# The last top-2 expert stage of a twelve-sublayer decoder: half the tokens routed earlier, fixed regions per expert

## The chip, the cores and the metric

The kernel runs on one core of a Trainium2 chip. The metric is the device time of one execution in microseconds (us); lower is better. Three runs of the kernel before took 828.32, 831.12 and 840.23 us, median 831.12 us.

## The reference

Four decoder layers of three sublayers each work on 1024 tokens (16 sequences of 64) of 128 features in float32; after each sublayer comes `x = layernorm(x + sublayer(x))`. The last two sublayers matter here: a 16-head cross attention (`x3` in the kernel), and a mixture of eight experts with two chosen per token:

```python
logits = xt @ Wg.T                                   # (1024, 8)
topk_logits, topk_idx = jax.lax.top_k(logits, 2)
w = jax.nn.softmax(topk_logits, axis=-1)
gates = jnp.zeros((T, N_EXPERTS)).at[rows, topk_idx].add(w)
h = gelu(einsum('th,ehi->tei', xt, W1) + b1)         # 128 -> 512 per expert
o = einsum('tei,eih->teh', h, W2) + b2               # 512 -> 128
y = einsum('te,teh->th', gates, o)
```

## The kernel before, in words

Tokens lie in eight tiles of 128 (tile t holds tokens 128t to 128t+127). Every sublayer is a chain of small steps per tile, each a few instructions on one engine: in `x3`, `v`/`q`/`k` project, `sc` scores, `ex` exponentiates, `tu` and `pt` transpose and copy back, `va` applies values (PE), `on` normalises (DVE), `fo` and `o` transpose the result, `y` is the output projection (PE), `re` adds the residual and takes its statistics (DVE), `rs` makes the reciprocal deviation (POOL), `fi` normalises (DVE), `x` transposes the new tile for the next stage (PE, then a copy on ACT). A planner (`chain_plan`) writes the order of these steps for each engine ahead of time; the change adds steps at fixed places of that order and moves none of the planner's own. Engines execute their list in order and meet by semaphores; a wait holds everything behind it on that engine.

The last expert stage (`top2_ffn` on each engine) then runs as follows. PE makes the router's logits (`logits`: one 128x8 matmul per tile; tiles 0 to 6 in one go just ahead of the last `x`, tile 7 behind it). DVE copies them, picks the first and second expert per token (`choose_first`, twice), and PE counts by matmuls with a triangular and an all-ones matrix how many tokens of each expert come before each token. DVE turns the counts into places (`slot3`), packed so that each expert's tokens start at a multiple of 128 behind the expert before. For that it needs the total counts of all tokens. POOL then scatters the token rows to DRAM (`slots3_x`): 16 indirect DMAs of 128 rows, each row 128 features and a row number. SP waits for all of them and loads the rows back as 23 blocks of 128 rows (three DMAs), and the row numbers in a fourth. DVE reads the 23 owners of the blocks into registers (`value_load`), and stages each block's weights by a register address (`fetch`, two copies). PE runs per block one transpose, four `up` matmuls and four `down` matmuls (each float32 matmul shows twice in the trace), ACT applies Gelu between, DVE copies the result, POOL scatters it to its tokens (`back3_y`). At the end SP loads those rows, and DVE and ACT add and normalise.

Ahead of this, long before it is used, SP zeroes the rows of `slots3_x` and later writes the row numbers of empty places into its last column; small tables that the ranks need are made by DVE in the middle of the program (`rank_tables`).

## Time and profile before

| what | value |
|---|---|
| profiled execution | 832.95 us; its span 831.0 us |
| busy: PE, PE weight loads, DVE, ACT, POOL | 679.0, 523.0, 586.3, 460.9, 435.3 us |
| mean granted PE clock | 0.869 |
| `x3` ends (last tile transposed) | 727.6 us into the span |
| scatters of the last stage | 736.8 to 758.2 us |
| first transposition of a loaded block | 761.0 us |
| expert loop | 761.0 to 811.2 us |
| rest: rows back, sum, normalisation, output | to 831.0 us |

Times of events count from the span's start. A busy PE is not a PE at its peak. In a timeline row, merged neighbours of one kind show as "x4"; idle time in brackets is the engine's own before that row, and what ended it. "issue" is time in which the engine waited for nothing that the profile shows.

### The profile page before, as it was taken

The numbers are of one execution on the slowest core, as the hardware profiler recorded it, in microseconds if no ns is written. First come the engines' busy times: TensorE is split into PE (matmuls) and PEld (weight loads), VectorE is DVE, ScalarE is ACT, GpSimd is POOL, SyncE is SP. The second block draws the span as 40 slices with busy tenths as digits, with TensorE's granted clock in tenths as the row PEclk, the third lists the DMA queues.
The fourth block names the chain that finished last, engine by engine and source line by source line (L and its number), as shares of the span: only waits on it lengthen the run. The fifth ranks groups of instructions, "written<-read, shape, count | busy, mean of one in ns | idle before, by whom it ended". The sixth has DMA issues, their size and how long they took to land.

```text
span 831.0 us, 21693 instructions
## 1 busy us (share of the span) xinstructions
PE 679.0 (82%) x8146; PEld 523.0 (63%) x8146; DVE 586.3 (71%) x1576; ACT 460.9 (55%) x1141; POOL 435.3 (52%) x579
## 2 busy tenths in 40 slices
PE   5888968899989996999967999859688899833990
PEld 2566625767867784777635776629565677622990
DVE  4876859799798765888568989435469789641554
ACT  2235737587876654877524765337347657322661
POOL 3268736677556532443327876135566667343450
PEclk8668968799999998999986999579889999855996
DMA  8068000000000000000019100031225460004002
GB/s 337 9 230 123 2 1 2 1 2 1 2 2 2 1 2 1 3 3 2 3 2 251 55 4 2 2 97 42 67 93 158 155 213 3 2 26 100 30 36 85
DMA packets 50804, 44.67 MB, mean 54 GB/s; under 512 B 15408, under 2 KB 41136, under 8 KB 50192
## 3 DMA queue, kind: packets, MB, share of 16 engines
q1 hardware_dynamic: 48464, 38.70, 16.8%
q0 software_dynamic: 2240, 4.60, 1.6%
q8 instruction: 67, 1.10, 0.6%
q14 instruction: 33, 0.27, 0.1%
HBM read 30.94 MB, written 12.36 MB: 52 GB/s over the span
## 4 chain that ended last, share of the span: by engine, by line
PE 49%; DVE 19%; POOL 9%; issue 9%; ACT 5%; DMA 5%; SPq 1%; DVEq 0%; ACTq 0%; POOLq 0%
PE bank L839 5%; PE bank L818 5%; PE bank L827 4%; PE bank L854 3%; PE bank L1002 3%; PE bank L1060 3%; PE bank L1067 3%; PE bank L910 2%; DVE pairs L1584 2%; DVE pairs L1580 2%; POOL slots_x L1955 2%; PE bank L887 2%; POOL sm L1897 2%; DMA rel_scratch<-G 2%; PE bank L749 1%
## 5 line engine op out<-in xcount | busy, mean ns | idle before, releaser
L1897 POOL TENSOR_TENSOR sm<-sm,mx 128x512 f32<-128x512 f32 x80 | 83.8, 1049 | 44.0 <-DVE mx L1534 43.4
L1158 ACT COPY pT<-bank 128x512 f32<-128x512 f32 x112 | 65.3, 583 | 38.4 <-PE bank L827 37.0
L1153 ACT ACTIVATE pr<-sm 128x512 f32<-128x512 f32 x112 | 70.1, 632 | 25.3 <-POOL sm L1897 24.4
L1892 POOL TENSOR_TENSOR pairs<-KS,quad 128x512 f32<-128x512 f32 x56 | 59.9, 1072 | 36.4 <-ACT KS L1135 36.4
L827 PE MATMUL bank<-W,pr 128*128 128x128 f32 x448 | 72.1, 285 | 8.1 <-ACT pT L1158 6.6
L1868 POOL TENSOR_SCALAR veps<-mv 128x1 f32<-128x1 f32 x104 | 25.1, 241 | 99.3 <-DVE mv L1469 99.2
L818 PE MATMUL bank<-pairs,Q 64*128 64x256 f32 x448 | 67.1, 420 | 2.0 <-DVE sm L1519 1.0
L839 PEld LDWEIGHTS bank<-VX,pT 64*64 64x64 f32 x3584 | 60.1, 139 | 13.0 <-issue 7.4
L839 PE MATMUL bank<-VX,pT 64*64 64x9 f32 (+1 forms) x3584 | 65.0, 203 | 2.4 <-ACT pT L1158 1.2
L1869 POOL TENSOR_TENSOR rstd<-veps,W 128x1 f32<-128x1 f32 x104 | 60.6, 583 | 8.7
L827 PEld LDWEIGHTS bank<-W,pr 128*128 128x128 f32 x448 | 51.0, 144 | 20.3 <-issue 10.9
L1534 DVE TENSOR_REDUCE mx<-sm 128x8 f32<-128x512 f32 x80 | 54.9, 686 | 2.8
L1168 ACT COPY XT<-bank 128x128 f32<-128x128 f32 x72 | 19.1, 266 | 58.6 <-PE bank L749 58.3
L1473 DVE TENSOR_SCALAR X<-res,mv,rstd 128x128 f32<-128x128 f32 x76 | 39.5, 520 | 15.2 <-POOL rstd L1869 14.9
L818 PEld LDWEIGHTS bank<-pairs,Q 64*128 64x128 f32 x448 | 41.2, 195 | 13.4 <-issue 7.2
L1141 ACT ACTIVATE Q<-bank,bqm,W 128x128 f32<-128x128 f32 x96 | 38.9, 458 | 9.1 <-PE bank L802 8.8
L887 PE MATMUL bank<-big,HT 128*128 128x512 f32 x64 | 38.3, 696 | 6.5 <-ACT big L1185 4.4
L749 PE MATMUL bank<-W,X 128*128 128x128 f32 x88 | 30.5, 347 | 14.1 <-DVE X L1473 13.1
L1531 DVE TENSOR_TENSOR sm<-bank,cap 128x512 f32<-128x512 f32 x48 | 32.8, 684 | 6.6 <-PE bank L818 6.0
L854 PE MATMUL bank<-WO,oT 128*64 128x128 f32 x384 | 34.6, 303 | 1.9 <-ACT oT L1162 1.4
L1912 POOL TENSOR_TENSOR big<-pairs 128x512 f32<-128x512 f32 x16 | 22.7, 1416 | 23.1 <-DVE pairs L1584 23.1
L1584 DVE TENSOR_TENSOR pairs<-big 128x512 f32<-128x512 f32 x32 | 32.5, 1015 | 0.0
(355 smaller groups left out, 1869.7 us busy)
## 6 DMA issues: line engine op xcount, KB each, us to landing
big<-gup SPq DMA_DIRECT2D x4, 1024.0 KB, 10.1
rel_scratch<-G SPq DMA_DIRECT2D x16, 256.0 KB, 2.9
W<-small SPq DMA_DIRECT2D x1, 3206.5 KB, 12.2
big<-early SPq DMA_DIRECT2D x2, 1557.0 KB, 8.4
slots_x<-zero SPq DMA_DIRECT2D x2, 1472.0 KB, 24.9
big<-down SPq DMA_DIRECT2D x8, 256.0 KB, 8.8
QM<-rel_scratch SPq DMA_DIRECT2D x16, 128.0 KB, 2.7
PM<-rel_scratch SPq DMA_DIRECT2D x16, 128.0 KB, 2.8
```

The costliest lines, as they stand in the source:

```text
L818: last = mm(ps[r][:, b * 256:(b + 1) * 256].rearrange("p (g k) -> p g k", g=4), Q[rows, q2 + b, :, :].rearrange("p c q -> p (c q)"), keys( ...
L827: last = pe.transpose(tile(ps, p), pr[:, u % 2, 4 * h + p, :, :].rearrange("p b k -> p (b k)"), ident)
L839: last = mm(ps[b][m, p * blk:(p + 1) * blk], pT[r, u % 2, p, m], V[r, 16 * s_ + 2 * p + c, :], start=True, stop=True)
L854: last = mm(ps[b * S:(b + 1) * S, 0:P], oT[:, t % 2, c * S:(c + 1) * S], WO[:, a["i"] % 4, b, c, :], start=(c == 0), stop=(c == 1))
L887: mm(fill(b_[0], (q_raw, k_raw)[i])[:, :], h, early_w(f"f{l}.wqkv", 512 * i, 512 * i + 512), start=True, stop=True).then_inc((fq_full, fk_ ...
L1153: act.activation(pr[:, u % 2, 4 * h:4 * h + 4, :, :].rearrange("p g b k -> p b g k"), sm[:, 2 * (u % 2) + h, :].rearrange("p (b g k) -> p ...
L1158: act.copy(pT[:, u % 2, 4 * h:4 * h + 4, :], bank[BK[f"tu{h}"]][:, :].rearrange("p (h n) -> p h n", h=4)).then_inc(pt_ready, 1)
L1534: dve.tensor_reduce(top, dst, AX.X, ALU.max).then_inc(mx_ready, 1)
L1584: return tt(M2[:, i, :].rearrange("p (h c d) -> p h c d", h=8, c=2), swapped, bc(table, [P, 8, 2, 32], 1), ALU.mult)
L1869: tt(rstd[:, i, :], veps[:, i, :], power, ALU.pow).then_inc(rstd_ready, 1)
L1892: tt(keys(u), bc(KS[:, u % 4, :], [P, 4, P], 1), bc(quad, [P, 4, P], 2), ALU.mult).then_inc(k_split, 1)
L1897: tt(v, v, bc(mx[:, slot, :], [P, 8, S], 2), ALU.subtract).then_inc(pcentered, 1)
```

## The change

The second experts' rows go to fixed regions, and the first four tiles are routed ahead.

- Each expert gets a fixed region of 1024 rows in `slots3_x` (11,136 rows with the spare ones; 2,944 before), so a place is `1024 * expert + rank` and needs no total. Places, row numbers and the filling grow with it: 87 blocks of 128 rows are zeroed and numbered where 23 were. Five DVE instructions are added to the tables in the middle of the program.
- Tiles 0 to 3: PE makes their logits behind `v` of tile 6 of `x3`, ACT copies them to SBUF behind the last `ex`; DVE picks the first expert behind `fi` of tile 4 (six instructions) and the second behind `v` of tile 7 (five); PE ranks them behind `x` of tile 5 by nine matmuls; DVE makes their eight columns of places behind `re` of tile 6 (three). POOL sends the first scatter behind `rs` of tile 6 and seven more behind `rs` of tile 7. ACT makes the two copies of each token tile right behind each `x` of `x3`, not in the last stage.
- Tiles 4 to 7 follow as before in `top2_ffn`, at half the size: a running sum over all choices (one scan of 128x128) and three rank matmuls; three DVE instructions make the places, and POOL sends the last eight scatters. A fourth matmul gives the totals, from which 12 DVE instructions make the blocks' owners and the address of each block's first row.
- SP reads 23 addresses into registers, and then issues 23 DMAs of 128 rows (row number included) in six groups with a semaphore each, where there were three and one for the numbers.
- DVE's 23 register loads are spread: five ahead of the sum with the experts' bias, seven behind it, eleven in the loop. ACT loads the Gelu table right behind the softmax's exponential.

PE's order at the end of `x3`, before; L749 is `x`, L846 `fo`, L854 `y`, L981 the logits:

```order
L749 MATMUL bank<-W,X 128x128 [waits o_ready,x_ready]
L846 MATMUL bank<-W,OB 128x128 [waits xt_ready,on_ready]
L854 MATMUL bank<-WO,oT 64x128 [waits y_used,wo_in,o_ready]
L854 MATMUL bank<-WO,oT 64x128 x3
L749 MATMUL bank<-W,X 128x128 [waits o_ready,x_ready]
L981 MATMUL bank<-W,XT 128x8 [waits on_ready,xt_ready]
L981 MATMUL bank<-W,XT 128x8 x6
L749 MATMUL bank<-W,X 128x128 [waits xt_ready,x_ready]
```

and with the change (L767 is `x`, L903 to L909 the early ranks, L864 `fo`, L872 `y`):

```order
L767 MATMUL bank<-W,X 128x128 [waits o_ready,x_ready]
L903 MATMUL bank<-QM,tri 128x64 [waits lg_ready,one_ready]
L908 MATMUL bank<-QM,ones 128x7x8
L908 MATMUL bank<-QM,ones 128x6x8
L908 MATMUL bank<-QM,ones 128x5x8
L908 MATMUL bank<-QM,ones 128x4x8
L908 MATMUL bank<-QM,ones 128x3x8
L908 MATMUL bank<-QM,ones 128x2x8
L908 MATMUL bank<-QM,ones 128x8
L909 MATMUL bank<-base,W 128x64
L864 MATMUL bank<-W,OB 128x128 [waits xt_ready,on_ready]
L872 MATMUL bank<-WO,oT 64x128 [waits y_used,wo_in,o_ready]
```

Between `x` of tile 5 and `fo` of tile 7 stand nine matmuls, and of the logits three tiles' are left further on instead of seven's.

SP's queue behind the experts' weights, before:

```order
L679 DMA big<-e3w 128x4x128 x4
L650 DMA pr<-slots_x 128x4x128 [waits scattered]
L650 DMA pr<-slots_x 128x12x128
L650 DMA sm<-slots_x 128x7x128
L651 DMA token_of<-slots_x 128x23x1
L687 DMA X<-back_y 128x4x128 [waits y_stored]
```

and with the change, from the last two of 23 register loads to the second of 23 block loads:

```order
L696 ISA x2
L696 TENSOR_LOAD first
L696 ISA x2
L700 REGISTER_ALU [waits scattered]
L700 DMA pr<-slots_x 128x129
L700 REGISTER_ALU
L700 DMA pr<-slots_x 128x129
```

The wait for the scatters now stands behind all 23 register loads, and each DMA behind a register operation.

POOL's order at the end of `x3`, before (L1868 and L1869 are `rs`):

```order
L1868 TENSOR_SCALAR veps<-mv 128x1 [waits var_ready]
L1869 TENSOR_TENSOR rstd<-veps,W 128x1 [waits pool_link]
L1955 DMA slots_x<-XB_id,slot 2944x129 [waits xs_ready,e3_in,slot_ready]
L1955 DMA slots_x<-XB_id,slot 2944x129 [waits xs_ready] x7
L1955 DMA slots_x<-WO,slot 2944x129 [waits xs_ready] x8
L1960 DMA back_y<-pT,token_of 4992x128 [waits block_ready,token_in]
```

and with the change (L1974 and L1975 are `rs`):

```order
L1974 TENSOR_SCALAR veps<-mv 128x1 [waits var_ready]
L1975 TENSOR_TENSOR rstd<-veps,W 128x1 [waits pool_link]
L2020 DMA slots_x<-XB_id,slot 11136x129 [waits xs_ready,e3_in,slot_ready]
L1974 TENSOR_SCALAR veps<-mv 128x1 [waits var_ready]
L1975 TENSOR_TENSOR rstd<-veps,W 128x1 [waits pool_link]
L2020 DMA slots_x<-VX,slot 11136x129 [waits xs_ready]
L2020 DMA slots_x<-XB_id,slot 11136x129 [waits xs_ready]
```

One scatter moved between `rs` of tiles 6 and 7; seven more follow with no wait for places.

```diff
+ROWS3 = NE3 * TOK + BLOCKS3 * P
+EARLY3 = MT // 2
+XG_GROUPS = [0, 1, 2, 3, 6, 10, BLOCKS3]
...
-    slots3_x = nc.dram_tensor("slots3_x", (BLOCKS3 * P, P + 1), F32, kind="Internal").ap()
-    back3_y = nc.dram_tensor("back3_y", (2 * TOK + BLOCKS * P, P), F32, kind="Internal").ap()
+    slots3_flat = nc.dram_tensor("slots3_x", (ROWS3 * (P + 1),), F32, kind="Internal").ap()
+    slots3_x = slots3_flat.rearrange("(r n) -> r n", n=P + 1)
+    back3_y = nc.dram_tensor("back3_y", (2 * TOK + ROWS3, P), F32, kind="Internal").ap()
...
+        XK = [VX32[:, :, :, :].rearrange("p a h d -> p (a h d)")[:, 0:EARLY3 * (P + 1)].rearrange("p (t n) -> p t n", t=EARLY3),
+              HT[:, :, :].rearrange("p b k -> p (b k)")[:, 0:EARLY3 * (P + 1)].rearrange("p (t n) -> p t n", t=EARLY3)]
+        hot = one[:, :, :].rearrange("p a b -> p (a b)").rearrange("p (e t k) -> p t k e", e=NE3, k=2)
+        XG3 = [pr[:, :, :, :, :].rearrange("p z i b k -> p (z i b k)")[:, i * (P + 1):(i + 1) * (P + 1)] for i in range(15)] + [
+            sm[:, :, :].rearrange("p z n -> p (z n)")[:, i * (P + 1):(i + 1) * (P + 1)] for i in range(BLOCKS3 - 15)]
...
-            sp.dma_start(slots3_x[:, 0:P].rearrange("(i p) n -> p i n", p=P), bc(zero[:, :], [P, BLOCKS3, P], 1)).then_inc(e3_in, 16)
+            sp.dma_start(slots3_x[:, 0:P].rearrange("(i p) n -> p i n", p=P), bc(zero[:, :], [P, ROWS3 // P, P], 1)).then_inc(e3_in, 16)
...
-            sp.dma_start(slots3_x[:, P:P + 1].rearrange("(i p) n -> p i n", p=P), token_of[:, 0:BLOCKS3].unsqueeze(2),
+            sp.dma_start(slots3_x[:, P:P + 1].rearrange("(i p) n -> p i n", p=P), fill3[:, :].unsqueeze(2),
...
+            sp.wait_ge(slot_ready, 5)
+            first = [sp.value_load(first3[0:1, j:j + 1], min_val=0, max_val=(ROWS3 - P) * (P + 1)) for j in range(BLOCKS3)]
             sp.wait_ge(scattered, 16 * MT * 3)
-            slots_in(slots3_x, BLOCKS3)
+            for j in range(BLOCKS3):
+                group = [j >= a for a in XG_GROUPS[1:]].count(True)
+                sp.dma_start(XG3[j], slots3_flat[bass.ds(first[j], P * (P + 1))].rearrange("(p n) -> p n", n=P + 1)).then_inc(xg3_in[group][0], 16)
...
+                        if name == "x3" and t == EARLY3 - 1:
+                            early_at = due.now(said)
+                        if name == "x3" and t == EARLY3 + 1:
+                            early_ranks()
+                    if step == "v" and name == "x3" and t == MT - 2:
+                        early_logits(early_at)
+            def early_logits(x_at):
+                pe.wait_ge(xt_ready, x_at)
+                ps = fill(0, lg_ready)
+                for t in range(EARLY3):
+                    last = mm(ps[:, t * NE3:(t + 1) * NE3], tile(XT, t), w("e3.r"), start=True, stop=True)
+                last.then_inc(logit_full, 1)
+            def early_ranks():
+                pe.wait_ge(one_ready, 3)
+                due(slot_ready)
+                ps = fill(0, slot_ready)
+                ranks = ps[:, 0:EARLY3 * NE2].rearrange("p (e t k) -> p e t k", e=NE3, k=2)
+                mm(ranks, tri[:, :], hot[:, 0:EARLY3, :, :].rearrange("p t k e -> p e t k"), start=True, stop=False)
+                ranks = ps[:, 0:EARLY3 * NE2].rearrange("p (e m) -> p m e", e=NE3)
+                for m in range(2 * EARLY3 - 1):
+                    n = 2 * EARLY3 - 1 - m
+                    own = hot[:, m // 2, m % 2, :]
+                    mm(ranks[:, m + 1:, :], ones[:, :], bc(own, [P, n, NE3], 1), start=False, stop=False)
+                mm(ps[:, 0:EARLY3 * NE2].rearrange("p (e m) -> p e m", e=NE3), ident, bc(base3[:, :], [P, NE3, 2 * EARLY3], 2),
+                   start=False, stop=True).then_inc(rank_full, 1)
...
-                pe.wait_ge(one_ready, 3)
-                due(slot_ready)
+                pe.wait_ge(one_ready, 4)
                 ps = fill(7, slot_ready)
-                chosen = one[:, :, :].rearrange("p t (k e) -> p e k t", k=2)
-                ps = ps[:, 0:2 * P].rearrange("p (i e k t) -> p i e k t", i=2, e=NE3, k=2)
-                mm(ps[:, 0, :, :, :], tri[:, :], chosen, start=True, stop=True)
-                mm(ps[:, 1, :, :, :], ones[:, :], chosen, start=True, stop=True).then_inc(rank_full, 1)
-                pe.wait_ge(one_ready, 4)
+                own = slice(2 * EARLY3, 2 * MT)
+                incl = two[:, :, :].rearrange("p a b -> p (a b)").rearrange("p (e m) -> p e m", e=NE3)
+                ranks = ps[:, 0:(MT - EARLY3) * NE2].rearrange("p (e m) -> p e m", e=NE3)
+                mm(ranks, ident, bc(base3[:, :], [P, NE3, 2 * (MT - EARLY3)], 2), start=True, stop=False)
+                mm(ranks, ones[:, :], incl[:, :, own], start=False, stop=False)
+                mm(ranks.rearrange("p e (t k) -> p e t k", k=2), trim[:, :], hot[:, EARLY3:MT, :, :].rearrange("p t k e -> p e t k"),
+                   start=False, stop=True).then_inc(rank_full, 1)
+                mm(fill(5, slot_ready)[:, 0:NE3], ones[:, :], incl[:, :, 2 * MT - 1], start=True, stop=True).then_inc(rank_full, 1)
+                pe.wait_ge(one_ready, 5)
...
+                        if name == "x3":
+                            act.copy(XB[:, t, :], X[:, t, :]).then_inc(xs_ready, 1)
+                            act.copy(XK[t // EARLY3][:, t % EARLY3, 0:P], X[:, t, :]).then_inc(xs_ready, 1)
+                    if step == "ex" and name == "x3" and t == MT - 1 and h == 1:
+                        act.wait_ge(logit_full, 2)
+                        act.copy(lg[:, 0:EARLY3, 0:NE3], bank[0][:, 0:EARLY3 * NE3].rearrange("p (t e) -> p t e", t=EARLY3)).then_inc(lg_ready, 1)
...
-                for t in range(MT):
-                    act.copy(XB[:, t, :], X[:, t, :]).then_inc(xs_ready, 1)
-                act.wait_ge(lg_ready, 3)
+                act.wait_ge(lg_ready, 5)
                 act.activation(col[:, 4, :], col[:, 3, :], ACT.Exp).then_inc(score_ready, 1)
-                for t in range(MT):
-                    act.copy(XK[:, t, 0:P], X[:, t, :]).then_inc(xs_ready, 1)
+                act.preload_act_table_set("gelu_and_others")
                 for hh in range(2):
...
+                link(tt(trim[:, :], tri[:, :], ones[:, :], ALU.subtract))
+                link(ts(base3[:, :], w("down8"), -float(TOK), float(TOK * NE3 - 1), ALU.mult, ALU.add))
+                link(dve.tensor_tensor_scan(fill3[:, :], ones[:, 0:ROWS3 // P], ones[:, 0:ROWS3 // P], 0.0, ALU.mult, ALU.add))
+                link(ts(fill3[:, :], fill3[:, :], float(P), upward[:, :], ALU.mult, ALU.add))
+                ts(fill3[:, :].bitcast(I32), fill3[:, :], float(TOK - P), None, ALU.add)
...
+                    if name == "x3":
+                        if step == "fi" and t == EARLY3:
+                            early_first()
+                        if step == "v" and t == MT - 1:
+                            early_second()
+                        if step == "re" and t == MT - 2:
+                            early_slots()
+            early = slice(0, EARLY3)
+            def early_first():
+                l8, one8 = lg[:, early, 0:NE3], hot[:, early, 0, :]
+                dve.wait_ge(lg_ready, 2)
+                link(choose_first(one8, l8, NE3, w("down8"), early, 2))
+                stt(l8, one8, -BIG, l8, ALU.mult, ALU.add).then_inc(lg_ready, 1)
+            def early_second():
+                dve.wait_ge(lg_ready, 3)
+                choose_first(hot[:, early, 1, :], lg[:, early, 0:NE3], NE3, w("down8"), early).then_inc(one_ready, 1)
+            def early_slots():
+                n = EARLY3 * NE2
+                place = sig[:, :, :].rearrange("p a b -> p (a b)")[:, 0:n]
+                by_e = lambda v: v.rearrange("p (e t k) -> p e t k", e=NE3, k=2)
+                dve.wait_ge(rank_full, 2)
+                link(tt(by_e(place), by_e(bank[0][:, 0:n]), hot[:, early, :, :].rearrange("p t k e -> p e t k"), ALU.mult))
+                link(dve.tensor_reduce(slotf[:, 0:2 * EARLY3], place.rearrange("p (e m) -> p m e", e=NE3), AX.X, ALU.add))
+                dve.tensor_copy(slot3[:, 0:2 * EARLY3], slotf[:, 0:2 * EARLY3]).then_inc(slot_ready, 1)
...
+                dve.tensor_tensor_scan(flat(two[:, :, :]), flat(newrow[:, :, :]), flat(one[:, :, :]), 0.0, ALU.mult,
+                                       ALU.add).then_inc(one_ready, 1)
                 tt(col[:, 3, :], col[:, 0, :], col[:, 2, :], ALU.subtract).then_inc(lg_ready, 1)
...
+                link(tt(start_of, over, bc(until, [P, BLOCKS3, NE3], 1), ALU.mult))
...
+                firstf = token_of[:, 0:BLOCKS3]
+                link(dve.tensor_reduce(firstf, start_of, AX.X, ALU.max))
+                link(tt(firstf, steps24[:, 0:BLOCKS3], firstf, ALU.subtract))
+                link(ts(whose[:, 0:BLOCKS3], whose[:, 0:BLOCKS3], float(TOK), -float(P), ALU.mult, ALU.add))
+                link(stt(firstf, firstf, float(P), whose[:, 0:BLOCKS3], ALU.mult, ALU.add))
+                ts(first3[:, :], firstf, float(P + 1), None, ALU.mult).then_inc(slot_ready, 1)
...
+                dve.wait_ge(slot_ready, 5)
+                start = []
+                def owner_of(j):
+                    start.append(dve.value_load(owner[0:1, j:j + 1], min_val=0, max_val=(NE3 - 1) * WIDE3))
+                for j in range(5):
+                    owner_of(j)
                 for hh in range(2):
                     dve.wait_ge(b2_full, hh + 1)
                     tt(total_y[:, NT * hh:NT * hh + NT, :], bank[hh][:, :].rearrange("p (t n) -> p t n", t=NT),
                        X[:, NT * hh:NT * hh + NT, :], ALU.add).then_inc(acc_ready, 1)
-                dve.wait_ge(slot_ready, 4)
-                start = [dve.value_load(owner[0:1, j:j + 1], min_val=0, max_val=(NE3 - 1) * WIDE3) for j in range(BLOCKS3)]
+                for j in range(5, 12):
+                    owner_of(j)
                 dve.wait_ge(e3_in, 16 * 12)
...
+                    if i + 12 < BLOCKS3:
+                        owner_of(i + 12)
...
+                    if step == "rs" and name == "x3" and t == MT - 2:
+                        pool.wait_ge(slot_ready, 3)
+                        pool.wait_ge(e3_in, 16 * 12)
+                        sent(0, 1)
+                if part == 2:
+                    sent(1, 2 * EARLY3)
...
+            def sent(a, b):
+                for m in range(a, b):
+                    t = m // 2
+                    row = XK[t // EARLY3][:, t % EARLY3, :] if m % 2 else XB_id[:, t, :]
+                    pool.wait_ge(xs_ready, MT + m + 1)
+                    pool.indirect_dma_start(slots3_x, bass.IndirectOffsetOnAxis(ap=slot3[:, m:m + 1], axis=0), row, None).then_inc(scattered, 16)
...
             chain(2)
-            pool.wait_ge(slot_ready, 3)
-            pool.wait_ge(e3_in, 16 * 12)
-            for m in range(2 * MT):
-                rows = XB_id if m < MT else XK
-                pool.wait_ge(xs_ready, MT + m + 1)
-                pool.indirect_dma_start(slots3_x, bass.IndirectOffsetOnAxis(ap=slot3[:, m:m + 1], axis=0), rows[:, m % MT, :],
-                                        None).then_inc(scattered, 16)
-            pool.wait_ge(token_in, 32)
+            pool.wait_ge(slot_ready, 4)
+            sent(2 * EARLY3, 2 * MT)
             for j in range(BLOCKS3):
                 pool.wait_ge(block_ready, BLOCKS + j + 1)
-                pool.indirect_dma_start(back3_y, bass.IndirectOffsetOnAxis(ap=token_of[:, j:j + 1].bitcast(I32), axis=0), YB[j],
+                pool.indirect_dma_start(back3_y, bass.IndirectOffsetOnAxis(ap=XG3[j][:, P:P + 1].bitcast(I32), axis=0), YB[j],
                                         None).then_inc(y_stored, 16)
```

## Rows read from the trace of the kernel before

**Rows 1.** Granted clock by stretch: from:to, length, busy us (instructions) per engine, PEclk, DMA share, GB/s.

```profile
718.00:728.00 10.00, 8.27 (x100) 6.27 (x100) 3.20 (x14) 1.46 (x7) 1.56 (x4) 0.58 0.01 2
728.00:761.00 33.00, 7.32 (x30) 5.71 (x30) 10.94 (x43) 4.40 (x19) 15.46 (x16) 0.50 0.15 45
...
770.00:810.00 40.00, 39.68 (x352) 39.49 (x351) 21.69 (x61) 27.28 (x104) 20.71 (x21) 0.99 0.09 34
```

**Rows 2.** The chain of waits, 755 to 762 us: start us, us, what.

```profile
755.89 2.28 DMA slots_x<-WO,slot
...
758.18 2.81 DMA pr<-slots_x
...
761.04 0.49 PE bank L1053
...
761.87 0.58 PE bank L1060
```

**Rows 3.** Line 1955: count, duration ns min/median/max, first and last start; its idle time.

```profile
L1955 POOL DMA_INDIRECT slots_x<-XB_id,slot x8: 954/958/1093, 736.8 to 745.8; - x8
L1955 POOL DMA_INDIRECT slots_x<-WO,slot x8: 954/958/959, 747.1 to 755.9; - x8
...
  issue: 4.6, 15
```

**Rows 4.** Timeline of the last tiles: start, us, engine, line, operation, [idle before <-releaser].

```profile
715.99 0.28 DVE L1565 TENSOR_TENSOR res<-bank,X 128x128 f32<-128x128 f32 x1
...
720.50 0.47 PE L749 MATMUL bank<-W,X 128*128 128x128 f32 x1
...
721.42 0.45 PE L846 MATMUL bank<-W,OB 128*128 128x128 f32 x1 [0.45 <-ACT XT L1168]
...
723.47 0.29 DVE L1565 TENSOR_TENSOR res<-bank,X 128x128 f32<-128x128 f32 x1 [0.61 <-PE bank L854]
...
724.11 3.15 PE L981 MATMUL bank<-W,XT 128*128 128x8 f32 x14 [0.35 <-ACT XT L1168]
...
724.69 0.56 POOL L1869 TENSOR_TENSOR rstd<-veps,W 128x1 f32<-128x1 f32 x1
```

**Rows 5.** Timeline, DVE from the logits' copy to the places' conversion.

```profile
728.55 0.23 DVE L1733 COPY QM<-bank 128x64 f32<-128x64 f32 x1 [2.92 <-PE bank L981]
...
736.35 0.17 DVE L1762 TENSOR_SCALAR slot<-slotf 128x16 int32<-128x16 f32 x1
```

**Rows 6.** Timeline, DVE and ACT around register loads, later and earlier stage; last its neighbour.

```profile
547.43 0.59 ACT L1260 ACTIVATE HT<-bank 128x512 f32<-128x512 f32 x1
...
552.01 1.56 ACT L1265 COPY cap<-big 128x768 f32 x2 [3.98 <-issue]
...
742.69 0.69 DVE L1777 TENSOR_TENSOR YF<-bank,X 128x512 f32<-128x512 f32 x1 [3.97 <-PE bank L1047]
...
744.40 0.69 DVE L1777 TENSOR_TENSOR YF<-bank,X 128x512 f32<-128x512 f32 x1 [1.01 <-PE bank L1047]
...
759.35 0.18 DVE L1783 COPY big<-W 128x32 f32<-128x32 f32 x1 [14.26 <-issue]
```

**Rows 7.** Timeline, the expert loop's first table load and one of its DVE steps.

```profile
764.48 1.28 ACT L1303 ACT_TABLE_LOAD   x1
...
773.91 0.32 DVE L1788 COPY b1s<-big 128x4 f32 x1 [0.88 <-PE bank L1067]
```

**Rows 8.** Timeline of SP's queue, four DMAs with other transfers under way.

```profile
659.86 4.48 SPq L674 DMA_DIRECT2D PM<-rel_scratch  x4
```

**Rows 9.** Timeline, DVE's tables in the middle chain and who waited for them.

```profile
427.99 0.42 DVE L1400 TENSOR_TENSOR_SCAN tri<-ones,W 128x128 f32<-128x128 f32 x1
...
430.83 0.45 PE L787 MATMUL bank<-W,YF 128*128 128x128 f32 x1 [4.92 <-DVE res L1562]
```

**Rows 10.** Two more stretches, columns as in the first group.

```profile
63.00:83.00 20.00, 16.67 (x270) 13.20 (x271) 13.93 (x38) 10.41 (x25) 17.13 (x27) 0.83 0.84 119
...
456.00:542.00 86.00, 79.03 (x1419) 60.03 (x1418) 67.87 (x194) 52.48 (x116) 52.30 (x68) 0.88 0.07 20
```

97 lines of the change are left out of this document (52 added, 45 removed).

## Prediction

> **What bounds the kernel now.** I read the chain of waits first, from its end. From 736.8 to 761.0 us PE does almost nothing for the result: POOL issues 16 scatters of 0.96 us, with 0.30 us of issue between them, 1.26 us each [rows 3]; the last starts at 755.89 and lands 2.28 us later; SP's first load lands 2.81 us after its issue, and PE begins the experts at 761.04, with the first up matmul at 761.87 [rows 2]. The reader is to see that this stretch is one engine's serial issue, not transfer: the DMA share is 0.15 [rows 1]. Behind it the loop is PE's: 39.68 us busy of 40 at 0.99 of full clock, the 2.4 GHz level, with 352 matmul records of which 17 make a block [rows 1], so 1.9 us a block. Ahead of it, `x3`'s last tiles run with PE at 0.58, mostly its lower level of 1.2 GHz [rows 1]. A change counts by how much earlier it brings the first up matmul.
>
> **The change part by part.** The sum is made against the profiled execution's 832.95 us, 1.8 us over the median of the three runs shown, 831.12.
>
> *Tables in the middle.* Five more DVE instructions. The longest of the old ones, a scan of 128x128, took 0.42 us, and PE waited 4.92 us for the residual behind these tables [rows 9], so they are on the path. At 0.17 to 0.42 each I take a sum of 1.4 us. **+1.4**, bounds 0.9 and 2.1.
>
> *Filling.* 8192 more rows are zeroed. While the old ones were written the DMA engines were 0.84 busy at 119 GB/s [rows 10]; 4.2 MB more last some 35 us, to about 118 us, and nobody in that stretch waits for a transfer. The column's 8192 more numbers delay the second-last experts' weights by perhaps 20 us; from 456 to 542 us, ahead of their use, the engines are 0.07 busy [rows 10]. Both at nothing; without that cover, up to 2.
>
> *`x3`'s end.* DVE picks the first expert of tiles 0 to 3 behind `fi` of tile 4. Six instructions at 0.23 us (the larger logits' copy took that, [rows 5]) start at about 716.05, and push `re` of tile 5 from 715.99 [rows 4] to 717.45; through DVE's order, `va` of tile 7 and `x` of tile 5 come some 1.6 us late, at 722.1 where 720.50 stood [rows 4]. The five instructions of the second pick lie in DVE's wait for that `va`. The early logits' eight passes fall in the same 1.6 us. Then the ranks: nine matmuls are 18 passes; 14 passes of the logits took 3.15 us, 0.225 each, at the lower clock [rows 4], so 4.05 us. `fo` of tile 7, at 721.42, 0.92 us after `x` of tile 5 [rows 4], now stands behind them and starts at 726.6, 4.5 us after it. `y`, `re` and `rs` of tile 7 follow it as before, so `re` moves from 723.47 to 728.7 and the end of `rs` from 725.25 [rows 4] to 730.45. DVE waits for the ranks ahead of `fi` of tile 6; that wait lies beside `fo` and `y` of tile 7, and only the first scatter (one of 16) gets in ahead. Three tiles' logits in place of seven give back four tiles' 1.8 us, of which 1.2 shows ahead of the last `x`.
>
> *Scatters.* After `rs` POOL has 15 left, without a gap: the late places are ready at about 738.3. I get that from the late logits' copy at 732.6, 4.0 us after 728.55, and 5.7 us of picks, scan, three small matmuls and three instructions where 7.97 passed before from copy to places [rows 5]; the early scatters occupy POOL until 739.6. So the first of the 15 starts at 730.8 and not 736.8 [rows 3], and one fewer is in the row: 6.0 + 1.26 = **-7.3**. The last lands at 750.9.
>
> *SP.* Its wait for the scatters stands behind 23 register loads, which can start at 741.6, when the addresses are there. No trace shows SP doing this, so two rows bound it. ACT passed 15 such loads in 3.98 us, 0.27 each; DVE passed 23 in 14.26 us, 0.62 each [rows 6]. They hide if one costs under (750.9 - 741.6) / 23 = 0.40 us. I take ACT's price: DVE's were read while POOL was in its scatters, whereas ACT, also beside scatters, was not slowed, and SP like ACT has nothing else in its queue. **0**; at DVE's price +5.0. The Trainium skill, DMA: Bandwidth & Descriptors, section Latency and other measured facts, puts a `tensor_load` at no less than about 600 ns; by that SP is ready at 755.4 and 4.5 us of the gain are gone. The trace has one row on either side of it.
>
> The first load is now 128 rows, not 512; I keep 2.86 us from issue to PE's start, perhaps 0.9 less.
>
> *DVE ahead of the loop.* The gates are ready at 743.1, the bias sums follow 4.0 and 5.7 us later as before [rows 6] and end at 749.5; seven loads at 0.27 to 0.62, the bias copy and the first fetch put the first weights at 752.6 to 755.0. The first up matmul's input is ready at 754.6. **0**, at worst +0.4.
>
> *Gelu's table*, 1.28 us [rows 7], lay in the first Gelu's path, but the second up matmuls run beside it and end only 0.4 us sooner than the Gelu: **-0.3**.
>
> *In the loop* DVE has eleven loads more. It idled 0.88 us per block [rows 7]; 0.62 fits. At one POOL period per load, 1.26 us, it would not, and eleven times 0.38 is +4.2. ACT's two copies per tile of `x3` replace 16 copies in the last stage; DVE is that stage's bound. **0**, at worst +1.
>
> Sum: 832.95 + 1.4 - 7.3 - 0.3 = 826.75; from the median, 831.12 - 6.2 = 824.9. I say **826**.
>
> **Rivals.**
> 1. *SP's register loads cost what DVE's do.* For: 0.62 measured, and the same instructions. Against: ACT's 0.27. First up matmul at 741.6 + 14.3 + 3.7 = 759.6, 2.3 us earlier than now; 832.95 - 2.3 - 0.3 + 1.4 = 831.75, from the median 829.9. Chance 0.25.
> 2. *SP becomes the bound: slower.* On top of rival 1, the last of the six groups holds blocks 10 to 22, so block 10 waits for all 23 DMAs. An issue cost SP 1.12 us where transfers crowded [rows 8]; 23 of them are 25.8 us, and with 2.3 us of landing the group is there at 755.9 + 28.1 = 784.0, while PE would take block 10 at 758.8 + 22.9 = 781.7 (ten blocks of 1.9 us and some 4 more at the lower clock). 831.75 + 2.3 = **834.0**. It decides from 0.9 us per issue. Against: blocks of 128 rows crowd little. Chance 0.12.
> 3. *PE is at its higher level in the ranks.* The dense run of small matmuls ends PE's pauses; at half the time per pass it gives 2 us more: 825, from the median 823. Chance 0.10.
> 4. *The early route hardly overlaps.* If the ranks or picks hold `x3` for twice what I reckon, another 5 us: 832. Chance 0.05.
>
> **How the numbers follow.** Forecast 0.48, rivals 0.25, 0.12, 0.10, 0.05. Own bounds of the forecast: from the tables -0.5 to +0.7, SP's smaller load -0.9, DVE +0.4, copies +1, the loop +4.2, and the scale between profile and median +-1; that is 822 to 830. The range is **820 to 834**: below for rival 3 with a shorter load, above for rivals 1 and 2. 2% of 831 is 16.6 us, about what a measurement of this kernel tells from no change. All cases lie within it. Faster by over 2% would need the whole 24 us between scatter and experts to shrink by two thirds: 0.04. Slower by over 2% would need SP's stream to cost twice rival 2's: 0.03. Same: 0.93.
>
> **What would show it.** Right: the 15 scatters start near 731 and end their landing near 751; nine matmuls of some 4 us between `x` of tile 5 and `fo` of tile 7; SP's first block load within a microsecond of the last landing; the loop still 1.9 us a block; the middle tables 1.4 us longer. Wrong: SP's first load at 756 (rival 1), a pause of PE before block 10 (rival 2), ranks in 2 us (rival 3), late places that come after 740, or DVE's idle time in the loop gone.

## The result

The changed kernel took a median of **848.01 us** over four runs (841.47 to 855.01), the kernel before 833.13 with the runs beside it. Ratio **1.0156**, 95% interval 1.0107 to 1.0205: slower by 13 us, though the interval reaches just past 2%, where 6 us less were forecast and 834 was the upper end of the range. Executions of one kernel lie up to some 3% apart, and ratios leave the disturbed ones out, but the profiles of `e4_loads_between`, `g1_three_rows`, `e7_all` and `f3_wide_six` below are of such ones (858.34, 858.03, 847.89 and 832.69 us), so of these four the rows are read and not the whole time. The profiled execution took 841.47 us (span 839.7, mean granted clock 0.864), 8.5 us more than the one of before, and is the fastest of its kernel's runs.

### The profile after

The first stretches to read are those of `x0`, where nothing of the change computes anything. Columns as in [rows 1]; the changed kernel, 63 to 105 us:

```profile
63.00:83.00 20.00, 15.80 (x193) 12.57 (x194) 12.00 (x33) 10.57 (x26) 16.91 (x27) 0.74 1.24 163
83.00:105.00 22.00, 18.43 (x327) 13.71 (x327) 15.29 (x42) 10.78 (x27) 12.07 (x18) 0.84 1.17 151
```

The kernel before had from 83 to 105 us:

```profile
83.00:105.00 22.00, 20.29 (x441) 15.62 (x439) 18.39 (x58) 14.97 (x38) 15.20 (x24) 1.00 0.01 3
```

PE passed 193 and 327 records where it had passed 270 [rows 10] and 441, at 0.74 and 0.84 of its clock where it had 0.83 and 1.00, and the DMA engines are still full. The timeline of PE shows how; changed kernel, 77 to 109 us (start, us, engine, line, operation, [idle before <-releaser]):

```profile
77.78 0.29 PE L857 MATMUL bank<-VX,pT 64*64 64x9 f32 x4 [0.99 <-issue]
...
83.99 1.12 PE L857 MATMUL bank<-VX,pT 64*64 64x9 f32 x64
...
85.95 0.65 PE L872 MATMUL bank<-WO,oT 128*64 128x128 f32 x6
...
89.78 0.59 PE L872 MATMUL bank<-WO,oT 128*64 128x128 f32 x2 [3.17 <-issue]
...
90.70 1.90 PE L857 MATMUL bank<-VX,pT 64*64 64x9 f32 x64
...
104.43 0.87 PE L857 MATMUL bank<-VX,pT 64*64 64x9 f32 x44
108.94 0.52 PE L857 MATMUL bank<-VX,pT 64*64 64x9 f32 x20 [3.64 <-issue]
```

One row of 64 matmuls stops ahead of its last 4, a row of 8 after 6, another of 64 after 44. Before, only the first of these is to be seen, and shorter:

```profile
76.66 0.29 PE L839 MATMUL bank<-VX,pT 64*64 64x9 f32 x4 [0.48 <-issue]
```

Their operands are those of the matmuls just done, so nothing that the program computes was missing; "issue" says the same. After the stall of 3.17 us the same 64 matmuls take 1.90 us, not 1.12: PE is back at its lower level of 1.2 GHz (granted clock 0.53 from 90 to 96 us). In the stretches of the two long stalls (84 to 90, 102 to 110) the DMA view has one packet of the instruction queue 8, among the data; from 84 to 90 us:

```profile
q1 hardware_dynamic: 1824, 0.93, 117.7%
q8 instruction: 1, 0.02, 1.5%
```

By itself that says little, since the stretch from 91 to 97 us has such a packet too and no stall. The trace has the start and end of each packet, though, and these settle it. All packets of queue 8 from 70 to 110 us, 16 KB each, in us:

| packet | before | PE's stall | after | PE's stall |
|---|---|---|---|---|
| 1 | 74.27 to 75.59 | 0.48, ends 76.66 | 74.89 to 76.12 | 0.99, ends 77.78 |
| 2 | 79.66 to 80.72 | none | 86.92 to 88.40 | 3.17, ends 89.78 |
| 3 | 85.20 to 86.56 | none | 96.07 to 97.44 | none |
| 4 | 92.77 to 94.08 | none | 106.56 to 107.68 | 3.64, ends 108.94 |

(Before has two more, from 97.44 and 104.36.) The second packet comes 7.3 us later than before, while PE, at the row of matmuls just ahead of it (81.50, before 79.42), was only 2.1 us late; the fourth comes 13.8 us later, with PE 8.2 us late. So the packets came some 5 us late against the program, and each of the three stalls ends 1.3 to 1.7 us after one is through.

The first FFN's first matmul then starts at 126.39 us, where it was 111.77: **14.6 us** are gone ahead of everything that I had costed, all but 0.6 of them behind 63 us.

The rest of the change went much as worked out. In the middle, DVE's five more rows and PE's wait behind them (4.92 in [rows 9]), and SP's columns:

```profile
445.00 0.28 DVE L1461 TENSOR_TENSOR trim<-tri,ones 128x128 f32<-128x128 f32 x1
...
447.25 0.45 PE L805 MATMUL bank<-W,YF 128*128 128x128 f32 x1 [6.23 <-DVE res L1620]
...
449.50 12.46 SPq L653 DMA_DIRECT2D slots_x<-token_of  x1
...
489.34 0.40 PE L857 MATMUL bank<-VX,pT 64*64 64x5 f32 x12 [1.77 <-issue]
```

The last row is one more stall of this kind: the columns put the second-last experts' weights off, and these are under way (share 1.10 from 480 to 490 us) when PE's next packet comes (486.62 to 487.84). All 13 profiles of the changed kernel and its variants have this stall, of 0.94 to 2.04 us, at the same matmul; none of the four profiles of the kernel before and its variants has it. No run moves the columns alone.

At the end of `x3` (compare [rows 4], and [rows 3] for the scatters), PE, POOL and DVE:

```profile
736.72 0.48 PE L767 MATMUL bank<-W,X 128*128 128x128 f32 x1
736.98 0.53 PE L903 MATMUL bank<-QM,tri 128*128 128x64 f32 x2
737.30 3.10 PE L908 MATMUL bank<-QM,ones 128*128 128x56 f32 x14
740.26 0.67 PE L909 MATMUL bank<-base,W 128*128 128x64 f32 x2
740.72 0.42 PE L864 MATMUL bank<-W,OB 128*128 128x128 f32 x1
...
744.75 1.15 POOL L2020 DMA_INDIRECT slots_x<-VX,slot  x1 [0.19 <-issue]
...
755.01 0.24 DVE L1861 TENSOR_SCALAR first<-token_of 128x23 int32<-128x23 f32 x1
...
762.63 0.96 POOL L2020 DMA_INDIRECT slots_x<-HT,slot  x1 [0.30 <-issue]
```

The ranks take 3.95 us, 4.05 forecast, and `fo` of tile 7 (L864) starts 4.00 us after `x` of tile 5, 4.5 forecast. The first of the 15 scatters starts at 744.75 and the last at 762.63. Then SP's queue, PE and DVE (compare [rows 2, 6]); and the parts of SP's register loads (count, duration ns min/median/max, first and last start):

```profile
766.60 0.18 DVE L1886 COPY big<-W 128x32 f32<-128x32 f32 x1 [3.62 <-issue]
...
768.95 8.63 SPq L700 DMA_DIRECT2D pr<-slots_x  x15
...
770.96 0.48 PE L1103 MATMUL bank<-W,pr 128*128 128x128 f32 x1 [8.71 <-DMA pr<-slots_x]
771.79 2.07 PE L1110 MATMUL bank<-pairs,cap 128*128 128x128 f32 x8 [0.35 <-ACT pairs L1352]
```

```profile
L696 SPq TENSOR_LOAD <-first x23: 261/268/485, 755.3 to 767.9; - x23
L696 SPq FUSED_REGOPS  x23: 147/147/187, 755.8 to 768.2; - x23
L696 SPq SEQ_ASSERT  x23: 18/18/29, 756.0 to 768.4; - x23
```

The addresses stand at 755.25, the last scatter lands 2.3 us after 762.63, at 764.9, and SP is through its loads only at 768.95: 13.7 us for 23, **0.60 us each**, 4.0 us behind the scatters. Each load proper takes 0.27 us; two more instructions follow it, 0.15 and 0.02 us, and from one load to the next it is 0.55 us for most of the 23.

Milestones, profile against profile (us):

| stretch | before | after | difference |
|---|---|---|---|
| start to the first FFN's first matmul | 111.8 | 126.4 | +14.6 |
| to SP's column fill | 320.9 | 322.7 | +1.8 |
| to SP's first `e3` weights | 231.7 | 227.5 | -4.2 |
| to SP's first block of `slots3_x` | 93.8 | 92.3 | -1.5 |
| to the first gather of `back3_y` | 55.9 | 53.6 | -2.3 |
| to the end | 16.9 | 17.2 | +0.2 |

The third line holds no step of the change except that the weights queue behind the columns, with that stall. Profiles of the changed kernel and its variants that leave this part alone lie between 227 and 252 us there, so I read nothing into it.

### The profile page after: what moved, and what is told of

It is laid out like the page before. It is cut to its first block, busy times and chain, and to the rows that moved or that the text cites. A ratio compares the mean times of both kernels' runs of the same rounds, so it can differ in the third digit from the quotient of the medians.

```text
span 839.7 us, 21898 instructions
## 1 busy us (share of the span) xinstructions
PE 689.0 (82%) x8168; PEld 531.5 (63%) x8168; DVE 592.1 (71%) x1597; ACT 462.3 (55%) x1142; POOL 436.4 (52%) x579
## 4 chain that ended last, share of the span: by engine, by line
PE 51%; DVE 21%; issue 11%; POOL 7%; ACT 4%; DMA 2%; SPq 1%; DVEq 0%; ACTq 0%; POOLq 0%
PE bank L836 5%; PE bank L857 5%; PE bank L845 5%; PE bank L872 3%; PE bank L1110 3%; PE bank L1049 3%; PE bank L1117 2%; PE bank L957 2%; DVE pairs L1670 2%; DVE pairs L1666 2%; PE bank L934 2%; DVE X L1531 1%; POOL sm L2003 1%; PE bank L812 1%; DVE sm L1589 1%
## 5 line engine op out<-in xcount | busy, mean ns | idle before, releaser
L845 PE MATMUL bank<-W,pr 128*128 128x128 f32 x448 | 74.9, 293 | 7.4 <-ACT pT L1208 6.2
L1974 POOL TENSOR_SCALAR veps<-mv 128x1 f32<-128x1 f32 x104 | 25.3, 244 | 103.4 <-DVE mv L1527 103.3
L836 PE MATMUL bank<-pairs,Q 64*128 64x256 f32 x448 | 68.9, 428 | 2.3 <-DVE sm L1589 1.0
L845 PEld LDWEIGHTS bank<-W,pr 128*128 128x128 f32 x448 | 52.9, 148 | 20.2 <-issue 11.0
L1975 POOL TENSOR_TENSOR rstd<-veps,W 128x1 f32<-128x1 f32 x104 | 60.7, 584 | 8.7
L1531 DVE TENSOR_SCALAR X<-res,mv,rstd 128x128 f32<-128x128 f32 x76 | 39.4, 518 | 13.8 <-POOL rstd L1975 13.6
L767 PE MATMUL bank<-W,X 128*128 128x128 f32 x88 | 30.7, 349 | 14.5 <-DVE X L1531 13.8
L872 PE MATMUL bank<-WO,oT 128*64 128x128 f32 x384 | 35.7, 307 | 4.9 <-issue 3.2
```

The lines of the kernel that those rows point to most:

```text
L836: last = mm(ps[r][:, b * 256:(b + 1) * 256].rearrange("p (g k) -> p g k", g=4), Q[rows, q2 + b, :, :].rearrange("p c q -> p (c q)"), keys( ...
L845: last = pe.transpose(tile(ps, p), pr[:, u % 2, 4 * h + p, :, :].rearrange("p b k -> p (b k)"), ident)
L872: last = mm(ps[b * S:(b + 1) * S, 0:P], oT[:, t % 2, c * S:(c + 1) * S], WO[:, a["i"] % 4, b, c, :], start=(c == 0), stop=(c == 1))
L1975: tt(rstd[:, i, :], veps[:, i, :], power, ALU.pow).then_inc(rstd_ready, 1)
```

## The experiments

**Is it the fill at all?** Take it away from `x0`, and put it alone into the kernel before.

`e1_late_zeros`, the changed kernel with:

```
-            sp.dma_start(slots3_x[:, 0:P]..., bc(zero[:, :], [P, ROWS3 // P, P], 1)).then_inc(e3_in, 16)
+            sp.dma_start(slots3_x[0:BLOCKS3 * P, 0:P]..., bc(zero[:, :], [P, BLOCKS3, P], 1)).then_inc(e3_in, 16)
...
+            sp.dma_start(slots3_x[BLOCKS3 * P:ROWS3, 0:P]...,            # behind the second layer's weights
+                         bc(zero[:, :], [P, ROWS3 // P - BLOCKS3, P], 1)).then_inc(e3_in, 16)
```

> The changed kernel, with the zeros of the last 64 of the 87 row groups of slots3_x written behind the second layer's weights (at about 460 us) and only the first 23 at 50 us, as in the kernel before; nothing is left out. The changed kernel's median is 848.0 us. Theory A (the larger fill at 50 to 105 us costs the 14 us by which everything from 118 us on is later, because TensorE's code, which comes over the same DMA engines, waits in it): L934's first row returns to about 112 us and the time falls by 12 to 15 us, to 833 to 836, if the same packets disturb nothing at 460 to 505 us; if they hold up code there too, it falls by 4 to 10 only. Rival B (the 12.5 us that SP needs to issue the column fill of 11136 words at 449 us, or the five operations more on the tables): no change, 846 to 850. Rival C (the clock or the code's place in memory, whatever the DMA does): no change.

Measured: 840.8 us, ratio 1.0116 (1.0009 to 1.0223). The first FFN starts at 115.2 us, 11.2 earlier than in the changed kernel (one stall of 2.21 us is left, in the small fill, where the kernel before with the same packets has 0.48); but from the column fill to the first blocks of `slots_x` it now takes 134.6 us, not 121.2. There PE now has three stalls, 0.94 (at 472.34, the place of the changed kernel's 1.77), 0.88 (491.72) and 4.31 us; the last, and the stretch:

```profile
500.50 0.38 PE L859 MATMUL bank<-VX,pT 64*64 64x5 f32 x4 [4.31 <-issue]
```

```profile
480.00:510.00 30.00, 23.39 (x372) 17.51 (x371) 15.81 (x48) 14.29 (x32) 15.86 (x18) 0.81 0.75 100
```

The fill takes stalls with it. That is A's second case; B and C said no change in `x0`. The ratio's interval overlaps that of the changed kernel, so the rows carry this, not the time.

`e2_before_many_zeros`, the kernel before with:

```
+    zeroed3_x = nc.dram_tensor("slots3_x", (87 * P, P + 1), F32, kind="Internal").ap()
+    slots3_x = zeroed3_x[0:BLOCKS3 * P, :]
...
-            sp.dma_start(slots3_x[:, 0:P]..., bc(zero[:, :], [P, BLOCKS3, P], 1)).then_inc(e3_in, 16)
+            sp.dma_start(zeroed3_x[:, 0:P]..., bc(zero[:, :], [P, 87, P], 1)).then_inc(e3_in, 16)
```

> The kernel before with one thing of the change: slots3_x has 87 row groups and all are zeroed at 50 us (only 23 are used); tables, column fill, choices and experts are as before. Kernel before: 833.1 us. Theory A (the larger fill costs x0 its 14 us): 845 to 849, with the first L887 row at 126 instead of 112 us. Rivals B and C (column fill and tables; the changed code itself): 831 to 835.

Measured: 842.3 us, ratio 1.0101 (1.0012 to 1.0190). The first FFN starts at 120.2 us, 8.4 later than before, and everything behind keeps the distance. Its stalls:

```profile
79.42 0.30 PE L840 MATMUL bank<-VX,pT 64*64 64x9 f32 x4 [1.99 <-issue]
...
90.77 0.58 PE L855 MATMUL bank<-WO,oT 128*64 128x128 f32 x2 [2.54 <-issue]
```

That is 8.4 of the 14.6 us: with two stalls, not three, it came out below A's 845 to 849. B and C (no change) fall: no new table, column or rank is in this kernel.

**Packets or bytes?** `e3_wide_zeros`, the changed kernel with:

```
-            sp.dma_start(slots3_x[:, 0:P]..., bc(zero[:, :], [P, ROWS3 // P, P], 1)).then_inc(e3_in, 16)
+            def zero_rows(slots, n, done):
+                own = slots.rearrange("(p i) n -> p (i n)", p=P)
+                a = n // 15 * 15 * (P + 1)
+                sp.dma_start(own[:, 0:a].rearrange("p (i n) -> p i n", n=15 * (P + 1)),
+                             bc(zeros, [P, n // 15, 15 * (P + 1)], 1)).then_inc(done, 16)
+                sp.dma_start(own[:, a:], zeros[:, 0:n % 15 * (P + 1)]).then_inc(done, 16)
```

(`zeros` is the buffer `G`, cleared by POOL at 6 us, so ACT waits for both fills ahead of the first FFN, and SP ahead of the columns. Both fills go this way, that of `slots_x` too. The text on record says 24 rows for `slots_x`; there are 23.)

> The changed kernel with the same bytes of zeros in few, long packets: POOL zeroes 15 rows of 129 numbers in a buffer that is free until the first FFN, and each partition writes its 87 (and 24) neighbouring rows in pieces of up to 15 rows, 768 pieces of up to 7.7 KB in place of 11136 of 512 bytes for slots3_x. The columns are written later as before. Theory A1 (code waits for the number of packets ahead of it, the fill is bound by packets): the fill is over before 75 us and the time falls by 14 to 18 us, to 830 to 834, since part of what the kernel before lost at 50 to 83 us goes too. A2 (bytes count, not packets): the fill's 7.3 MB take as long, fall under 4 us. Rivals B and C: no change, 846 to 850.

Measured: 829.9 us, ratio 0.9955 (0.9915 to 0.9995): 2% under the changed kernel, 17 us. PE has no such stall in `x0`, and the first FFN starts at 111.7:

```profile
63.00:83.00 20.00, 16.07 (x276) 12.20 (x274) 14.96 (x37) 11.45 (x27) 18.64 (x30) 0.91 0.80 329
83.00:105.00 22.00, 20.12 (x438) 15.38 (x436) 18.62 (x60) 15.16 (x38) 15.03 (x24) 1.00 0.01 3
```

The fill does PE no harm. A1 holds. The 329 GB/s are a mean over a stretch of which the last microseconds are idle; from 70 to 75 us the engines moved 415, in the changed kernel 197. PE's first packet came in the middle of the fill (73.67 to 74.75) with no stall at all, and the others when it was over or nearly so. So a fill of long packets harms less and also ends sooner, and this run doesn't part the two. The next ones vary the packets for the same bytes.

`g0_after_beside` is the changed kernel beside them; `g1_three_rows` is `e3_wide_zeros` with pieces of 3 rows in place of 15 (`n=3 * (P + 1)`), in both fills; `g2_half_rows` is the changed kernel, its smaller fill as it was, with

```
+            for c in range(2):
+                sp.dma_start(slots3_x[:, c * S:(c + 1) * S]..., bc(zero[:, 0:S], [P, ROWS3 // P, S], 1)).then_inc(e3_in, 16)
```

> The changed kernel beside the next two, on one chip. Every theory: 1.010 to 1.016 of the kernel before, TensorE's two stalls of 3 to 4 us at about 87 and 106 us, the first FFN's first row (L934) at 122 to 127 us.

> The changed kernel with its zeros in pieces of 3 rows (1548 bytes), so 3712 pieces in place of 11136 for slots3_x and 981 in place of 2944 for slots_x; the same bytes. Theory A (the packets count, at about 5 ns each of all 16 engines together): the fill ends at about 72 us in place of 105, at most one stall under 1.5 us, the first FFN at 112 to 114 us, 0.993 to 0.999 of the kernel before. Rival B (bytes or the presence of any fill count): the first FFN at 120 us or later, 1.005 or more.

> The changed kernel with each row of slots3_x zeroed as two half rows of 256 bytes by two DMAs: 22272 packets, the same bytes, everything else the same. Theory A (the packets count): the fill lasts until about 150 us, TensorE meets one to three more fetches in it, the first FFN starts at 130 to 140 us and the first FFN is disturbed as well: 10 to 20 us slower than the changed kernel, 1.025 to 1.035 of the kernel before. Rival B (bytes count): the fill ends near 106 us as in the changed kernel and the time is the same to 2 us.

PE's first stalls in `g1_three_rows`, and in `g2_half_rows`:

```profile
77.56 0.29 PE L866 MATMUL bank<-VX,pT 64*64 64x9 f32 x4 [1.23 <-issue]
...
87.39 0.38 PE L881 MATMUL bank<-WO,oT 128*64 128x128 f32 x2 [0.96 <-issue]
```

```profile
83.09 0.38 PE L860 MATMUL bank<-VX,pT 64*64 64x9 f32 x4 [5.31 <-issue]
98.08 0.58 PE L875 MATMUL bank<-WO,oT 128*64 128x128 f32 x2 [6.14 <-issue]
120.99 0.81 PE L860 MATMUL bank<-VX,pT 64*64 64x9 f32 x20 [6.34 <-issue]
134.88 1.89 PE L860 MATMUL bank<-VX,pT 64*64 64x9 f32 x63 [4.12 <-issue]
```

| packet of the large fill | packets | stalls of PE, us | first FFN | ratio to before |
|---|---|---|---|---|
| up to 7740 B (`e3`) | 768 | none | 111.7 | 0.9955 (0.9915 to 0.9995), first set |
| 1548 B (`g1`) | 3712 | 1.23, 0.96 | 115.0 | 1.0039 (0.9995 to 1.0083) |
| 512 B (`g0`) | 11136 | 0.68, 3.86, 2.28 | 127.0 | 1.0127 (1.0034 to 1.0219) |
| 256 B (`g2`) | 22272 | 5.31, 6.14, 6.34, 4.12 | 143.9 | 1.0405 (1.0336 to 1.0474) |

The bytes of the large fill are the same in all four to 1%, so B falls. `g1` came out less good than A's 0.993 to 0.999: its fill took 35.8 us to land, not 22. `g2` came out worse than A's 1.025 to 1.035 and 130 to 140 us. The stalls come at the same places of PE's program (4 matmuls ahead of the end of a row of 64, 2 ahead of the end of a row of 8, the last 20 of a row of 64). The second and third are the longer the more packets there are; the first is not in that order (1.23 us with 1548 B, 0.36 to 0.99 with 512 B in the changed kernel's profiles). So what PE waits for comes at fixed places of its code and has to pass the packets: its code. Every stall bears that out. The nine profiles with fills of short packets (`before`, `after`, `e1`, `e2`, `e4`, `a0`, `g0`, `g1`, `g2`) have 23 such stalls beside a fill, and 13 profiles have the one beside the weights; each of the 36 ends 1.07 to 2.00 us after a packet of queue 8 is through. Nothing in the trace says that queue 8 is PE's; this timing does. It fits the Trainium skill, Runtime: NRT & Kernel Launch, section Instruction fetch mechanics: each sequencer refills its instructions in blocks over a DMA queue of its own, 16 KiB at a time, and the packets here are of 16,384 B. The page calls the cost mostly hidden; the rows here show 0.4 to 6.3 us for a block that PE waits for while short packets fill the engines.

`a0_after_again` is the changed kernel once more, in the second set of runs.

> The changed kernel itself once more, since runs of one kernel spread by 5 us and it has had only three undisturbed ones. Every theory: 1.010 to 1.020 of the kernel before, as its first runs gave 1.0156; if it comes out at 1.005 or less, the loss at 50 to 105 us is a matter of chance in when the code is fetched, and the other comparisons must be read by ratio and by row only. The two stalls of TensorE of about 3 us at about 87 and 105 us should be there again.

Measured 852.9 beside 843.4, ratio 1.0103 (1.0026 to 1.0180), with stalls of 0.81 and 2.75 us and the first FFN at 121.9. The second stall of about 3 us that was expected is missing. So the loss is there each time, in varying size: the three sets give 1.010 to 1.016.

**SP's loads.** `e4_loads_between`, the changed kernel with:

```
-            first = [sp.value_load(first3[0:1, j:j + 1], ...) for j in range(BLOCKS3)]
+            for j in range(12):
+                first_of(j)
             sp.wait_ge(scattered, 16 * MT * 3)
             for j in range(BLOCKS3):
+                if j >= 12:
+                    first_of(j)
```

> The changed kernel with 12 of SP's 23 register loads ahead of its wait for the scatters and the other 11 each ahead of its own block's DMA. Theory A (the loads cost SP 0.6 us each and so end 4 us behind the last scatter's landing): first block's DMA at about 765 us in place of 769 on the profile's time, the time falls by 3 to 4 us, to 844 to 845. Rival B (the first take waits for something else that is ready only then, such as the weights' copy or the first transfer after the scatters): no change, under 1 us. Rival C (the loads between the DMAs, at 1.1 to 1.3 us for a block's pair, or waits of later blocks, hold up the loop): slower by 1 us or more.

Measured: 836.3 us, ratio 1.0014 (0.9970 to 1.0057). The last scatter starts at 783.23 and the first block at 785.87, 2.64 us later, where it was 6.32; and from there to the first gather it takes 53.5 us, as in the changed kernel.

```profile
785.87 10.57 SPq L708 DMA_DIRECT2D pr<-slots_x  x15
```

A by the rows: 3.7 us back, and B and C fall. The time fell by more than that, 7 to 12 us by the ratios, and that surplus stays open. The stalls of `x0` are there in its profile (0.36, 3.59 and 3.51 us), but this is of its slowest execution; whether the faster ones had them isn't shown.

In the second set the loads took longer. In `a0_after_again` the addresses stand at 762.01 and the first block goes at 782.71: 20.7 us. The chain there:

```profile
765.04 1.40 SPq L696
766.45 0.71 issue
767.16 0.72 SPq L696
...
772.91 0.26 SPq L696
773.17 0.03 issue
...
773.46 0.26 SPq L696
```

It isn't that each load is dearer. From 772.91 on they follow each other at 0.55 us, as in the profile of the result; but between 763.6 and 772.8 only four are begun, with most steps of SP some 0.7 us long or twice that. So it is one disturbed stretch, 7 us longer than its loads need. DVE's first five loads beside it keep their 0.6 us each, and then DVE sits idle until 772.91. `g0_after_beside` took 20.5 us in the same way, `f2_wide_again` 13.7. The texts on record put this down to the chip, but the second and the third set ran on the same one. What causes the stretch isn't known; it is in all profiles of the second and fourth sets in which SP has such loads, and in none of the first and third.

**The ranks.** `e6_few_ranks`, the wide kernel with:

```
-                for m in range(2 * EARLY3 - 1):
-                    ...
-                    mm(ranks[:, m + 1:, :], ones[:, :], bc(own, [P, n, NE3], 1), start=False, stop=False)
+                mm(ranks, ones[:, :], incl, start=False, stop=False)
+                mm(..., trim[:, :], hot[:, 0:EARLY3, :, :]..., start=False, stop=True).then_inc(rank_full, 1)
...
+                dve.tensor_tensor_scan(flat(two[:, :, :]), flat(newrow[:, :, :]), flat(one[:, :, :]), 0.0, ALU.mult, ALU.add)
```

> The changed kernel with the wide fill, and the early ranks in 3 matmuls of 64 columns in place of 17: a scan over the early choices (one more operation of VectorE in its step) gives the running sums that 15 of the matmuls added up, as the late half does it already. Theory A (each of the 18 passes at 0.22 us lies on TensorE's path to x3's last tile): L903 to L909 shrink from 3.95 us to under 1 us and everything behind is 3.0 to 3.3 us earlier: 3 us less than the wide kernel, 826 to 827 on its scale. Rival B (VectorE, not TensorE, is the bound at x3's end, so the passes are hidden): under 1 us less. Rival C (the scan delays VectorE's chain and the ranks): no less, or more.

Its PE rows:

```profile
733.24 0.47 PE L776 MATMUL bank<-W,X 128*128 128x128 f32 x1
733.51 0.53 PE L913 MATMUL bank<-base,W 128*128 128x64 f32 x2
733.83 0.63 PE L914 MATMUL bank<-QM,ones 128*128 128x64 f32 x2
734.26 0.63 PE L915 MATMUL bank<-QM,trim 128*128 128x64 f32 x2
...
736.52 0.48 PE L776 MATMUL bank<-W,X 128*128 128x128 f32 x1
```

The matmuls are three in place of nine, each shown twice; the text on record counts 17. They take 1.38 us, not A's under 1. From one transpose to the next it is 3.28 us, where the changed kernel has 5.83 (736.72 to 742.55): 2.55 us less, under A's 3.0 to 3.3. The whole is 840.8, ratio 0.9977 (0.9935 to 1.0020), beside `before` at 843.4; the wide kernel had 0.9955 in the first set, without the 7 us of SP's disturbed stretch that this profile has. Across the sets 2.5 us can't be shown, so A stands by the rows alone.

`e5_before_wide` and, in a third set, `f1_before_wide`: the kernel before with the wide fill.

> The kernel before with long packets for its two fills (24 and 23 rows of 129 numbers of each partition in pieces of up to 15 rows), nothing else. Theory A (a fill of short packets holds up TensorE's code only where it lasts until a fetch): the kernel before's fill was over at 78 us and its one stall 0.5 us, so 0 to 2 us less, 831 to 835; then the change's own worth without its fill is the ratio of the wide changed kernel to this one, about 0.996 to 0.998. Rival B (the gain of the wide fill over the changed kernel has nothing to do with the number of row groups): this falls by as much, 14 us or more.

> The kernel before with the wide fill, again, as the foot of a chain of one-step comparisons on one chip (its first four runs gave 0.988 with an interval of 0.979 to 0.996 against the kernel before). Theory A (short packets cost the kernel before nearly nothing, its stall was 0.5 us): 0.997 to 1.002. Rival B (they cost it a slower clock and small stalls in x0 too): 0.985 to 0.993.

Measured 0.9876 (0.9791 to 0.9961), from three executions, then 0.9953 (0.9915 to 0.9991) from twelve. So the kernel before gains some 4 us by it (0.8 to 7 by the second interval), which lies between A and B. Where it gains them isn't shown: in the two profiles the first FFN starts at 110.70 and 111.92 us, where it was 111.77.

`e7_all` has the wide fill, few ranks and 12 loads ahead.

> Wide fill, few ranks, and SP's loads split as 12 ahead of the wait and 11 among the DMAs. Theory A (the three costs add up): 17 us for the fill, 3 for the ranks, 4 for the loads against the changed kernel, so 822 to 824, ratio 0.985 to 0.99 of the kernel before. Rival B (the places of the late tiles, not SP's loads, set when the scatters end and the first take waits for them): the loads give back nothing where the ranks are already shorter: 826.

Measured 0.9864 (0.9820 to 0.9907), 11 us under `before`. In its profile the last scatter's start and the first block are still 6.9 us apart, since the 12 loads ahead of the wait take 14.3 us there, the disturbed stretch among them.

**One step at a time**, in the third set, each against the same runs of the kernel before:

> The changed kernel with the wide fill. Against the kernel before with the wide fill this is the change's worth without its fill. Theory A (the prediction's local terms hold, with SP's loads at 0.60 us: 7.3 us for the scatters, 2.3 in the loop and 0.3 for the table gained, 1.4 for the tables and 4 for the loads lost): 3 to 6 us less than the kernel before with the wide fill on a chip like the first, where SP's loads take 13.7 us; on one where they take 20.7, as on the second chip, nothing or 2 us more. Rival B (choices and ranks inside x3 cost as much as the scatters gain): 2 to 5 us more, whatever the loads cost.

> The same with 6 of SP's register loads ahead of its wait for the scatters and 17 each ahead of its own block's DMA. Theory A (all that the loads cost is that they end behind the scatters): the first block's DMA follows the last scatter's start by 2.3 to 2.7 us, in place of 6.3 or 13.3: 4 us less than the wide kernel on a chip like the first, up to 10 less on one like the second. Rival B (a load and a DMA of each block are then paced at 1.2 us or more and late for the loop's 1.9 us a block): first matmul early, the loop's end not, less than 2 us.

> The same with the early ranks in 3 matmuls (6 passes for 18). Theory A: 2.5 us less than the kernel with 6 loads, which is what the rows of x3's end gave at the lower clock (5.6 us from tile 6's transpose to tile 7's, then 3.0). Rival B (TensorE's clock falls to its lower level the earlier in x3's end, and takes it back): 0 to 1 us less. With all three the kernel should be 0.97 to 0.98 of the kernel before.

| kernel | ratio to before | last scatter's start to first block, us |
|---|---|---|
| `f1_before_wide` | 0.9953 (0.9915 to 0.9991) | 2.29 |
| `f2_wide_again`, the change with the wide fill | 0.9923 (0.9884 to 0.9963) | 6.33 |
| `f3_wide_six`, and 6 loads ahead | 0.9898 (0.9852 to 0.9945) | 2.64 |
| `f4_all_six`, and few ranks | 0.9883 (0.9836 to 0.9930) | 2.50 |

The change without its fill is worth 0.3%, 2.5 us, where A said 3 to 6 for 13.7 us of loads; the loads give 2.1 (4 expected), the ranks 1.2 (2.5 expected). The signs are those of A, but every step is smaller than expected and less than the intervals, so none of the three is shown by the times. All together the kernel is at 0.988 and not the 0.97 to 0.98 on record. It beats both all the same: 825.45 us, 1.2% under the kernel before and, across the sets, 2 to 3% under the changed one.

## Why the prediction was wrong

- **Filling, the step that failed.** It put the zeros "at nothing", because "nobody in that stretch waits for a transfer". I had looked for tiles that wait for data. What waits is PE's own code, which no row of a wait names: it stands as "issue" and breaks a row of matmuls in two. Cost 14.6 us in the profile, 8 to 16 over the five profiles with this fill in `x0`, against "up to 2". Some 7.3 us are the stalls themselves (0.99 + 3.17 + 3.64, before 0.48) and 0.6 stood already ahead of them. Most of the rest is the lower clock behind them: at the same row of matmuls PE is 6.0 us late just behind the second stall and 8.2 ahead of the third, 12.2 behind that one and 14.6 at the end, with no stall between. The trace of before held the sign: the engines were full, and PE had one "issue" stall of 0.48 us in the fill, on a matmul of a row of 64. The 0.84 busy and 119 GB/s [rows 10] were read as the fill's own; they are a mean over a stretch of which nearly the last 6 us are idle, and inside the fill it was 1.27 and 168 (70 to 75 us). So the fill ended at 108 us and not at 118.
- **The columns** were put at nothing too, and in sum there it held: SP spent 12.46 us, and the stretch behind is no longer (121.2 us, before 121.8), though it has the one stall of 1.77 us beside the delayed weights, again of code, that "nothing" had no place for.
- **Tables**: forecast 1.4, PE's wait grew by 1.31.
- **`x3`'s end and the scatters**: passes at 0.22 us as reckoned, 3.95 us together. Counted from `fi` of tile 4, which came 13.8 us later than before, the first of the 15 scatters is at 730.9 (forecast 730.8), and the last starts 7.1 us earlier than it would have (forecast 7.3 to the landing).
- **SP**, the second step that failed: the choice of ACT's price was wrong, and DVE's right: 0.60 a load. That is rival 1, whose 5.0 came out as 4.0 us. I had argued DVE's row away by the scatters beside it. But the two rows are not of the same instructions, which neither the forecast nor rival 1 saw. ACT's loads are written without bounds (`act.value_load(owner[0:1, j:j + 1])`), DVE's and SP's with `min_val` and `max_val`, and each of these is followed by two instructions more. In the kernel before:

```profile
L1282 ACTq TENSOR_LOAD <-owner x15: 272/280/340, 547.0 to 551.4; - x15
...
L1781 DVEq TENSOR_LOAD <-owner x23: 296/301/637, 744.4 to 758.7; - x23
L1781 DVEq FUSED_REGOPS  x23: 183/183/216, 745.1 to 759.1; - x23
```

  The load proper takes 0.27 to 0.30 us on all three engines; ACT's follow each other at 0.31 us, DVE's at 0.61, SP's at 0.55. (The 0.27 for ACT is too low: the 3.98 us are only its idle part of 4.7.) No run here has SP's loads without bounds. The Trainium skill, DMA: Bandwidth & Descriptors, section Latency and other measured facts, has the floor of about 600 ns; that came near for a load with its bounds, and ACT's 15 at 0.31 lie under it.
- **Rival 2** (SP as the bound) did not happen: 15 block DMAs went out in 8.63 us, 0.58 each, against the 0.9 at which it decides. Nor did **rival 3**, the granted clock in the ranks was 0.50, nor **rival 4**, the scatters began as reckoned.
- **SP's smaller load** gave its 0.9 us: 2.84 from issue to the first up matmul, before 3.69. That is part of the 2.3 us by which the loop is shorter; 0.3 were forecast for the table, and the rest isn't traced. **DVE ahead of the loop** was ready at 767.75, ahead of the rows, as forecast, and eleven loads in the loop cost nothing that shows.
- With 14.6 for the fill and 4.0 for the loads the sum is 826.75 + 18.6 = 845.4, against the profile's 841.5 and the median's 848.0. What the profile lies below the sum is about the third line of the milestones (-4.2), which has no known reason. The terms of the last stages came out within about a microsecond but for SP's. The rivals were all about these stages; none asked what the added transfer would do to an engine that waits for no data.

## What to carry to other kernels

A long fill of short packets is not free because no tile waits for it: PE here drew its unrolled code past the same packets, and stalled in "issue" in the middle of a row of like instructions. Look for a transfer whose share is near 1 at a low rate, and for the instruction queue's packet just ahead of each such stall's end. Write the bytes in few long packets, or not at all, before asking where to put them. Cost a register load by one written the same way, with or without bounds, and issue a block's load just ahead of its own DMA rather than all ahead of a common wait.

## What the runs showed of the hardware

- PE stalled for its code while short packets were under way, at the same places of the program: not with 7.7 KB, 1.0 to 1.2 us with 1.5 KB, 0.4 to 4.3 with 512 B, 4.1 to 6.3 with 256 B. The kernel before had one such stall in its fill, of 0.48 us; beside the second-last experts' weights (share 1.10) 13 profiles had one of 0.94 to 2.04.
- Each of these 36 stalls ended 1.07 to 2.00 us after a packet of 16 KB of the instruction queue 8 was through.
- The long stalls were followed by a stretch at the lower level of PE's clock (1.90 us for 64 matmuls that had taken 1.12; granted clock 0.50 to 0.60 behind those of 3.17 and 3.64 us). Of the short ones some were not: behind 0.48 in `before`, 0.68 in `g0_after_beside` and 0.96 in `g1_three_rows` it stayed at 1.00.
- A register load took 0.27 to 0.30 us on SP, DVE and ACT. With its bounds it took SP 0.55 and DVE 0.61 from one to the next, without them ACT 0.31. In the second and fourth sets SP had one disturbed stretch of some 9 us among its loads, beside which DVE's wait for the bias sum was 9.5 us in place of 3.96.
- While the large fill of zeros was under way, the DMA engines moved 415 GB/s in pieces of up to 7.7 KB (70 to 75 us), 277 in 1.5 KB (75 to 80), 139 to 181 in 512 B and 77 to 98 in 256 B (both from 75 to 100, by stretches of 5 us).
